# First attention of an eight-layer kernel: second half of the queries first, chunks projected and handed on inside the loop

## The chip, the core and the metric

The kernel runs on one core of a Trainium2 chip. The metric is the device time of one execution in microseconds; the median of three runs is given. Engines: TensorE (PE; its weight loads are PEld), VectorE (DVE), ScalarE (ACT), GpSimd (POOL) and SyncE (SP), which issues the DMAs.

## The reference, cut to what matters

Eight layers follow each other on x (2 batches of 1024 tokens, 128 features), each with a layer norm ahead of it and added back: four attentions and four feed-forward layers. The change lies in the first attention and in its hand-over to the first feed-forward layer.

```python
B, S, D = hidden_states.shape            # 2, 1024, 128
H, hd = (NUM_HEADS, HEAD_DIM)            # 16, 8
qkv = hidden_states @ w_attn + b_attn
scores = einsum('bhqd,bhkd->bhqk', q, k) * hd ** -0.5
# delta = key - query: -log(delta + 1) where delta > 0, 0 where 0, -inf where delta < 0
scores = scores + _power_law_mask(S)
attn = softmax(scores, axis=-1)
out = einsum('bhqk,bhkd->bhqd', attn, v) @ w_proj + b_proj
```

A query thus sees itself and the keys behind it. The second half of the queries (512 to 1023) sees only keys of the second half; the first half sees both. The next layer is a gated feed-forward: `silu(x @ wg.T) * (x @ wu.T) @ wd.T` with 384 hidden features.

## The kernel before

**Chunks and norm.** x lies in 4 chunks of 512 tokens (NC = 4, QC = 2 per batch). A `Norm` stands ahead of each layer: VectorE makes statistics (line 94, 98) and xn (line 106), GpSimd the root (lines 117, 119) and adds the output bias to x (line 136), TensorE turns xn (line 152), ScalarE copies it to xnT (line 165) and, for the feed-forward layer, rounds a high part (168), of which GpSimd makes the low part (125). `Part.ready` says after which addition the next norm may start; TensorE waits for all four chunks before it turns the first.

**Projection and stacks.** For each chunk TensorE projects q and k (line 449) and v (453). Q and k are split into three bf16 parts: high on ScalarE (575), rest on VectorE (638), mid on ScalarE (580), low on VectorE (653). SP stores them to DRAM (line 380, seven DMAs a chunk) and loads them back stacked, 48 rows a head (line 405, four DMAs a unit). One tile `parts` holds the parts of two chunks, so ScalarE waits for the stores of batch 0 before chunk 2. The order on SP's queue is: stores of chunks 0 and 1, stacks of units 0 to 2, stores of chunks 2 and 3, then the rows of maxima (line 394) and further stacks.

**Units.** A unit is 4 heads of one batch; there are 8 (UNITS). For each, the maximum over the keys of every query is found first: TensorE makes scores by query in 24 pieces (diagonal: lines 475, 481; behind: 487), VectorE reduces each (671). 8 of the pieces belong to the second half of the queries. VectorE then joins and splits the negated maxima into three bf16 parts (682 to 690), TensorE turns them (495), ScalarE copies them (619), SP moves them as rows under the stacked queries (394). Then the scores by key (line 511; logarithm of the weight added by 518, 519, or a mask by 523), exp on ScalarE (606), the weight on GpSimd for part of them (420), the product with V (540), the numerators copied (614), turned (549) and divided on VectorE (698, 701) into `o`, which is m.xn.

**The order of work** is one list, `schedule()`, that each engine follows for its own kinds. Its clock is the half: one pair of heads of one key block of one half of the queries. A unit has 12 groups (NG) and 24 halves (HALVES); the widths of its groups are 512 x5, 384, 256, 128 columns for the first half of the queries and then 512, 384, 256, 128 for the second. The product with V comes 7 halves after its scores. All 24 maxima of unit 0 stand ahead of the loop; those of unit u + 1 are spread over 24 halves that end 10 before unit u does (unit 1: 14 halves). Banks 4 to 6 of PSUM go round among scores by key, turned maxima and turned numerators.

**The end.** After the loop the four chunks are turned (560), copied (629), projected (565), added to x (712), and the norm of the next layer follows each. The next layer's gates are lines 765 and 766, their product on VectorE line 803; its weights are widened on ScalarE (752, 753) when the first attention has left it.

## Time and profile before

| what | us |
|---|---|
| median of 3 runs | 1101.84 |
| lowest, highest | 1100.96, 1110.02 |
| the profiled execution | 1110.22 |
| its span, first to last instruction | 1108.4 |
| mean granted clock of TensorE in it | 0.883 of full |

One execution was profiled. A row of the stage table gives the busy time of each engine in a stretch, with its instructions in brackets, and the granted clock (1.00 is 2.4 GHz, 0.50 is 1.2 GHz; between them the stretch had both). A row in order of time gives start and length in us; several instructions of one kind in a row are merged, with their count, and the bracket names the idle time ahead of them and what ended it.

### The profile page before, as it was taken

The numbers are of one execution on the slowest core, as the hardware profiler recorded it, in microseconds if no ns is written. First come the engines' busy times: TensorE is split into PE (matmuls) and PEld (weight loads), VectorE is DVE, ScalarE is ACT, GpSimd is POOL, SyncE is SP. The second block draws the span as 40 slices with busy tenths as digits, with TensorE's granted clock in tenths as the row PEclk, the third lists the DMA queues.
The fourth block names the chain that finished last, engine by engine and source line by source line (L and its number), as shares of the span: only waits on it lengthen the run. The fifth ranks groups of instructions, "written<-read, shape, count | busy, mean of one in ns | idle before, by whom it ended". The sixth has DMA issues, their size and how long they took to land. (4 is left out here: it accounts for less than half of the span.)

```text
span 1108.4 us, 17915 instructions
## 1 busy us (share of the span) xinstructions
PE 901.9 (81%) x6590; PEld 615.8 (56%) x6590; DVE 646.5 (58%) x1444; ACT 431.0 (39%) x1024; POOL 513.7 (46%) x462
## 2 busy tenths in 40 slices
PE   4559999999998877357899699995999996399993
PEld 2113334333333356255566588995896766289992
DVE  6756676767661065879687655778102666643334
ACT  2334665566555542113211285774344211032221
POOL 5435978887886832053222343655200001146661
PEclk9658999999997988758799698998899998599996
DMA  5700110111000000001000000211000000266775
GB/s 168 232 1 2 30 31 4 28 30 30 3 1 23 1 22 8 0 15 39 1 2 1 7 19 15 73 69 53 25 1 1 1 10 29 70 186 215 218 211 145
DMA packets 38747, 55.95 MB, mean 50 GB/s; under 512 B 6682, under 2 KB 26146, under 8 KB 38534
## 3 DMA queue, kind: packets, MB, share of 16 engines
q1 hardware_dynamic: 36166, 49.70, 14.8%
q0 software_dynamic: 2496, 5.12, 1.7%
q8 instruction: 54, 0.88, 0.3%
q14 instruction: 31, 0.25, 0.1%
HBM read 43.66 MB, written 10.94 MB: 49 GB/s over the span
## 5 line engine op out<-in xcount | busy, mean ns | idle before, releaser
L671 DVE TENSOR_REDUCE arena<-ps 128x2 f32<-128x1024 f32 (+2 forms) x192 | 177.4, 955 | 86.7 <-PE ps L487 55.4
L420 POOL TENSOR_TENSOR arena<-arena 128x1024 f32<-128x1024 f32 (+3 forms) x105 | 201.1, 1952 | 37.8 <-ACT arena L606 37.8
L606 ACT ACTIVATE arena<-ps 128x512 f32<-128x512 f32 (+3 forms) x320 | 138.7, 489 | 90.7 <-PE ps L519 56.1
L117 POOL TENSOR_SCALAR vareps<-meanvar 128x4 f32<-128x4 f32 x32 | 8.0, 250 | 213.7 <-DVE meanvar L98 213.7
L511 PE MATMUL ps<-arena 51*128 51x512 bf16 (+3 forms) x384 | 91.5, 348 | 18.0 <-ACT arena L606 7.1
L511 PEld LDWEIGHTS ps<-arena 51*128 51x128 bf16 x384 | 26.6, 94 | 107.1 <-ACT arena L606 61.4
L2084 PE MATMUL ps<-arena 128*128 128x128 f32 x624 | 78.2, 280 | 0.0
L152 PE MATMUL ps<-ident,xn 128*128 128x128 f32 x128 | 26.6, 358 | 59.2 <-DVE x L930 19.9
L2084 PEld LDWEIGHTS ps<-arena 128*128 128x128 f32 x624 | 74.8, 196 | 0.0
L420 POOL TENSOR_TENSOR xnT<-xnT,arena 128x1024 f32<-128x1024 f32 (+1 forms) x28 | 52.6, 1899 | 42.2 <-ACT xnT L606 42.2
L487 PE MATMUL ps<-arena 48*128 48x512 bf16 (+3 forms) x320 | 56.1, 347 | 17.5 <-DVE arena L671 14.8
L540 PE MATMUL ps<-arena 128*9 128x512 f32 (+3 forms) x640 | 69.0, 508 | 0.0
L1410 PEld LDWEIGHTS ps<-arena 128*128 128x128 f32 x512 | 63.8, 196 | 2.9
L1410 PE MATMUL ps<-arena 128*128 128x128 f32 x512 | 63.7, 279 | 0.0
L165 ACT ACTIVATE xnT<-ps 128x512 f32<-128x512 f32 x32 | 18.8, 595 | 110.6 <-PE ps L152 103.6
L2250 DVE TENSOR_TENSOR arena<-ps,arena 128x512 f32<-128x512 f32 x39 | 27.0, 692 | 58.2 <-PE ps L2084 57.3
L2044 POOL DMA_INDIRECT expert_rows<-arena x39 | 38.6, 989 | 40.9 <-ACT arena L2132 40.3
L2031 POOL DMA_INDIRECT arena<-token_rows,arena x39 | 38.0, 975 | 37.2 <-DVEq L2232 24.7
L152 PEld LDWEIGHTS ps<-ident,xn 128*128 128x128 f32 x128 | 20.2, 188 | 62.8 <-issue 43.4
L2118 ACT ACTIVATE arena<-ps 128x512 f32<-128x512 f32 x39 | 23.3, 597 | 71.0 <-PE ps L2084 70.9
L1461 ACT ACTIVATE arena<-arena 128x128 f32<-128x128 f32 x128 | 37.9, 297 | 31.2 <-DVE arena L1579 31.2
L1275 DVE TENSOR_TENSOR arena<-ps,arena 128x512 f32<-128x512 f32 x64 | 39.6, 681 | 17.3 <-PE ps L1157 17.3
(343 smaller groups left out, 2043.2 us busy)
## 6 DMA issues: line engine op xcount, KB each, us to landing
arena<-in_L_ffn_w SPq DMA_DIRECT2D x39, 512.0 KB, 3.7
arena<-scratch SPq DMA_DIRECT2D x32, 192.0 KB, 4.0
arena<-in_L_ffn_w SPq DMA_DIRECT2D x16, 256.0 KB, 3.3
scratch<-arena SPq DMA_DIRECT2D x12, 256.0 KB, 4.0
arena<-expert_rows SPq DMA_DIRECT2D x8, 256.0 KB, 5.0
scratch<-arena SPq DMA_DIRECT2D x4, 384.0 KB, 5.3
scratch<-arena SPq DMA_DIRECT2D x12, 128.0 KB, 4.1
x<-in_x SPq DMA_DIRECT2D x4, 256.0 KB, 3.8
```

The lines of the kernel that those rows point to most:

```text
L152: last = nc.tensor.transpose(m.ps[:, self.banks[n % len(self.banks)], j * P:(j + 1) * P], m.xn[:, n * TPC + j, :], m.ident[:, :])
L420: nc.gpsimd.tensor_tensor(e, e, weight[:, at:at + k].unsqueeze(1).broadcast_to([P, 2, k]), ALU.mult).then_inc(weighed, 1)
L487: mm = nc.tensor.matmul(m.ps[:, bank + e, 0:wd], qs[rows, u % BUFS, pair, at * P:(at + 1) * P], ks[rows, u % BUFS, pair, j:j + wd], start= ...
L511: mm = nc.tensor.matmul(m.ps[:, bank, 0:wd], ks[rows, u % BUFS, p, kt * P:(kt + 1) * P], qs[rows, u % BUFS, p, CH * qc:CH * qc + wd], star ...
L540: mm = nc.tensor.matmul(m.ps[PAD * h:PAD * h + HD + 1, 7, 0:wd], vones[:, b * TB + kt, u % G * GH + h, :], probs(u * NG + n)[:, h, 0:wd], ...
L606: nc.scalar.activation(probs(g)[:, 2 * p + e, 0:wd], m.ps[:, BANK[h, e], 0:wd], ACT.Exp, scale=SCALE).then_inc(exps, 1)
L671: nc.vector.tensor_reduce(out, scores, AX.X, ALU.max, negate=True).then_inc(max_set, 1)
L1275: nc.vector.tensor_tensor(at[:, t % 2, g, :].rearrange("p (j q) -> p j q", q=P), m.ps[:, g, :].rearrange("p (j q) -> p j q", q=P), causal[ ...
L1410: mm = nc.tensor.matmul(m.ps[:, 4 + n % 2, j * P:(j + 1) * P], hT[:, n % 2, f, j * P:(j + 1) * P], w2c[:, e % 2, f, :], start=False, stop= ...
L2031: nc.gpsimd.indirect_dma_start(xg[:, s % RING, :], None, m.token_rows, bass.IndirectOffsetOnAxis(ap=token_i[:, s:s + 1], axis=0),).then_in ...
L2044: nc.gpsimd.indirect_dma_start(m.expert_rows, bass.IndirectOffsetOnAxis(ap=target_i[:, s:s + 1], axis=0), y[:, s % RING, :], None,).then_i ...
L2084: mm = nc.tensor.matmul(m.ps[:, 2 * (s % 2) + half, f * P:(f + 1) * P], w_up[:, s % WBUFS, at + f * P:at + (f + 1) * P], xgT[:, s % 2, :], ...
```

## The change

- **Order of the queries.** Units 0 to 3 (batch 0) take the second half of the queries first, units 4 to 7 the first half. The pieces are listed with the second half first.
- **Maxima in halves.** For units 0 and 1 the maxima are split, turned, copied and moved in two turns (TURNS): first blocks 4 to 7, then 0 to 3. Only 8 pieces of unit 0 stand ahead of the loop. Its other 16 are due in halves 0 to 5, with the split at 6, the turning at 7 and the copy at 8. Unit 1: 2 pieces at 6, 4 at 7, 2 at 8 and 9, 16 in 10 to 21. Unit 2: all 24 in halves 22 to 37 (before 14 to 37). Later units as before.
- **Chunks inside the loop.** Four new kinds of work: turn_o, take_o, project, add. They use the rotating banks 4 to 6. Chunks 0 and 1 come after unit 3 (chunk 1 twelve halves later), chunk 2 after the first half of the queries of unit 7, chunk 3 at the end. With each addition VectorE does the statistics of that chunk and the normalisation of the chunk before it; GpSimd does the root 10 halves after the last product, or behind its last weighing.
- **Hand-over.** The next layer's chunk 0 is turned right behind the last product with V, and copied and split on ScalarE behind the last numerators. `wait_xnT` of that layer no longer waits for all chunks. The roots of its norm are taken as they come, at most one chunk ahead of the low part; that of chunk 3 falls between the low parts of chunks 1 and 2. The next layer's norm uses banks 3, 7, 6, 7.
- **Start.** The identity and three small loads (w, bqk, bv) are issued behind the first chunk of x, with semaphores of their own; TensorE waits for these and not for all seven loads. The first norm normalises each chunk behind the statistics of the next. The parts of batch 1 have a place of their own, in ring slots 2 and 3, so ScalarE doesn't wait for the stores of batch 0; it waits for the stores of batch 1 at group 3 instead.
- **SP's queue.** Stores of chunks 0 and 1, first three stores of chunk 2, stack of unit 0, the other stores, rows of unit 0, stacks of units 1 and 2, then rows and stacks as before.
- **Smaller.** `masked` lies in ring slot 0 and is made ahead of the logarithm, the scaling by 1 / SCALE goes from GpSimd to ScalarE, oT has a tile of its own.

```diff
     def vector(self, dve):
         while self.counted_stats < NC:
             self.statistics(dve, self.counted_stats)
+            if self.k == 0 and self.counted_stats >= 2:
+                self.normalise(dve, self.counted_xn)
...
         for c in range(NC):
-            ts = slice(c * TPC, (c + 1) * TPC)
-            pool.wait_ge(m.ln_var, 2 * self.value(c))
-            nc.gpsimd.tensor_scalar(m.vareps[:, ts], m.meanvar[:, ts, 1], LN_EPS, None, ALU.add).then_inc(m.ln_rstd, 1)
-            pool.wait_ge(m.ln_rstd, 2 * self.value(c) - 1)
-            nc.gpsimd.tensor_tensor(m.rstd[:, ts], m.vareps[:, ts], m.power[:, ts], ALU.pow).then_inc(m.ln_rstd, 1)
-        for c in range(NC):
+            while self.counted_roots < (min(c + 2, NC) if self.before.ahead else NC):
+                self.root(pool, self.counted_roots)
...
-        if self.turned == 0:
-            pe.wait_ge(*self.before.ready[NC - 1])
-            if self.k == 0:
-                pe.wait_ge(m.set_up, 2)
-                pe.wait_ge(m.consts_in, 16 * (2 + len(BIASES)))
+        if self.turned == 0 and not self.before.ahead:
+            pe.wait_ge(*self.before.ready[0 if self.k == 0 else NC - 1])
+        self.turn(pe, min(c + 2, NC))
...
+    ORDER = [tuple(range(QC)) if u >= (B - 1) * G else tuple(reversed(range(QC))) for u in range(UNITS)]
+    TURNS = [turn for u in range(UNITS) for turn in ([(u, TB - TPC, TB, 0, LATER), (u, 0, TB - TPC, LATER, NP)] if u < 2 else [(u, 0, TB, 0, NP)])]
...
-    def window(u):
-        return (0, HALVES - 10) if u == 1 else ((u - 1) * HALVES - 10, (u - 1) * HALVES + HALVES - 10)
+    def windows():
+        yield 0, LATER, NP, 0, 6
+        yield 1, 0, 2, 6, 7
+        yield 1, 2, 6, 7, 8
+        yield 1, 6, LATER, 8, 10
+        yield 1, LATER, NP, 10, HALVES - 2
+        yield 2, 0, NP, HALVES - 2, 2 * HALVES - 10
+        for u in range(3, UNITS):
+            yield u, 0, NP, (u - 1) * HALVES - 10, u * HALVES - 10
+
+    SPLIT_AT = [None, 6, 10, HALVES - 2] + [u * HALVES - 10 for u in range(2, UNITS)]
...
+    LATE = {c: 12 * (c == 1) for c in range(NC)}
+    ROOT_AT = {c: 2 * (u * NG + LAST[u][r]) + 2 * LAG + 10 + LATE[c] for c, (u, r) in FINISHED.items()}
...
-        yield from (("max", 0, n) for n in range(NP))
+        yield from (("max", 0, n) for n in range(LATER))
         yield from ((what, 0, 0) for what in ("split", "turn_max", "take_max"))
...
+                            for what, late in (("turn_o", 5), ("take_o", 6), ("project", 7)):
+                                due.setdefault(at + 2 * LAG + late + LATE[c], []).append((what, u, c))
+                            due.setdefault(at + 2 * LAG + 8 + LATE[c], []).insert(0, ("add", u, c))
...
+        for c in range(QC):
             for j in range(2):
+                store(c, j)
+        store(QC, 0)
+        stack(sp, 0)
+        store(QC, 1)
+        for c in range(QC + 1, NC):
+            for j in range(2):
+                store(c, j)
         maxima(sp, 0)
+        for u in range(1, BUFS):
+            stack(sp, u)
...
+    def maxima(sp, s):
+        u, lo, hi, _, _ = TURNS[s]
+        sp.wait_ge(mrows_set, s + 1)
+        if s and TURNS[s - 1][0] == u:
+
+            sp.wait_ge(s_mm, 2 * u * HALVES + 1)
...
+        def turn_outputs(u, c):
+            pe.wait_ge(o_set, u * QC + FINISHED[c][1] + 1)
+            bank = free_bank(("turn_o", u, c))
+            for j in range(TPC):
+                mm = nc.tensor.transpose(m.ps[:, bank, j * P:(j + 1) * P], o[:, c * TPC + j, :], m.ident[:, :])
+            mm.then_inc(o_turned, 1)
...
+            if what == "times_v" and (u, n) == (UNITS - 1, NG - 1):
+                turn_next(pe, 1)
...
+            if g == 3 and p == 0:
+                act.wait_ge(parts_out[B - 1], OUT)
...
+            if what == "take_num" and (u, n) == (UNITS - 1, QC - 1):
+                copy_next(act, 1)
...
+        def add(u, c):
+            dve.wait_ge(y_mm, c + 1)
+            dve.wait_ge(m.biased, norm.biased_value(c))
+            xs = m.x[:, c * TPC:(c + 1) * TPC, :]
+            nc.vector.tensor_tensor(xs, m.ps[:, BANK["project", u, c], :].rearrange("p (j d) -> p j d", d=D), xs, ALU.add).then_inc(x_done, 1)
+            after(dve, c)
```

## Rows read from the trace of the kernel before

**Rows 1.** the page: each engine's busy us (share of span) xinstructions

```profile
PE 901.9 (81%) x6590; PEld 615.8 (56%) x6590; DVE 646.5 (58%) x1444; ACT 431.0 (39%) x1024; POOL 513.7 (46%) x462
```

**Rows 2.** stages: stretch, length, PE PEld DVE ACT POOL busy, clock, DMA share, GB/s

```profile
39.60:63.00 23.40, 12.30 (x70) 3.23 (x68) 21.51 (x26) 1.98 (x3) 11.12 (x4) 0.59 0.50 160
63.00:70.70 7.70, 1.02 (x8) 0.74 (x8) 1.29 (x6) 2.30 (x2) 0.00 (x0) 0.50 0.01 3
70.70:92.00 21.30, 17.52 (x82) 5.42 (x84) 13.20 (x14) 9.61 (x18) 16.25 (x7) 0.59 0.00 1
92.00:105.00 13.00, 11.60 (x104) 4.73 (x100) 10.29 (x16) 5.42 (x15) 4.94 (x4) 1.00 0.00 1
143.90:182.50 38.60, 35.99 (x292) 14.26 (x290) 27.21 (x35) 22.37 (x52) 31.77 (x16) 1.00 0.09 22
386.70:403.40 16.70, 8.78 (x65) 7.61 (x61) 12.39 (x52) 6.99 (x12) 6.47 (x10) 0.86 0.10 26
```

**Rows 3.** order of time, the start; columns: start, length, engine, line, operation

```profile
13.23 1.97 PE L152 MATMUL ps<-ident,xn 128*128 128x128 f32 x8 [13.23 <-DMA arena<-in_L_attn_before]
...
15.03 2.65 PE L449 MATMUL ps<-xnT,arena 128*128 128x512 f32 x4
...
19.82 8.84 SPq L380 DMA_DIRECT2D scratch<-arena  x14
...
31.01 0.60 ACT L165 ACTIVATE xnT<-ps 128x512 f32<-128x512 f32 x1 [6.91 <-DMA scratch<-arena]
...
38.60 0.59 PE L475 MATMUL ps<-arena 128*128 128x512 bf16 x2 [1.08 <-DVE arena L650]
```

**Rows 4.** order of time, last maxima of unit 0 to first scores by key

```profile
54.83 1.04 PE L475 MATMUL ps<-arena 128*128 128x512 bf16 x2 [0.90 <-DVE arena L671]
...
62.94 0.39 DVE L682 TENSOR_TENSOR arena<-arena 128x28 f32<-128x28 f32 x2
...
66.61 43.70 SPq L394 DMA_DIRECT2D arena<-arena  x8
...
70.72 0.61 PE L511 MATMUL ps<-arena 51*128 51x512 bf16 x2 [5.18 <-DMA arena<-arena]
```

**Rows 5.** order of time of ScalarE, line 619 of unit 2 and unit 6

```profile
143.88 1.01 ACT L619 ACTIVATE arena<-ps 12x1024 bf16<-12x1024 bf16 x1 [1.90 <-PE ps L495]
...
296.43 1.01 ACT L619 ACTIVATE arena<-ps 12x1024 bf16<-12x1024 bf16 x1 [1.89 <-PE ps L495]
```

**Rows 6.** TensorE's busy time in four units by lines 487, 475, 481

```profile
143.90:296.40 152.50, 26.93 (x160) 1.00 0.09 22
...
143.90:296.40 152.50, 9.64 (x32) 1.00 0.09 22
...
143.90:296.40 152.50, 6.35 (x128) 1.00 0.09 22
```

**Rows 7.** order of time, last product with V to the next layer

```profile
384.39 2.34 PE L540 MATMUL ps<-arena 128*9 128x512 f32 x32
...
387.94 1.93 PE L560 MATMUL ps<-ident,xn 128*128 128x128 f32 x16
...
388.44 0.29 DVE L701 TENSOR_TENSOR xn<-ps,arena 128x128 f32<-128x128 f32 x1
...
389.71 1.06 PE L565 MATMUL ps<-arena 128*128 128x128 f32 x8
...
400.96 1.04 POOL L119 TENSOR_TENSOR rstd<-vareps,power 128x4 f32<-128x4 f32 x1
...
406.93 0.63 PE L765 MATMUL ps<-rounded 128*128 128x512 f32 x1
```

**Rows 8.** order of time of line 106 without and with GpSimd beside it

```profile
400.48 1.08 DVE L106 TENSOR_SCALAR xn<-x,meanvar,rstd 128x128 f32<-128x128 f32 x4
...
401.97 2.50 POOL L125 TENSOR_TENSOR rounded<-xnT,rounded 128x512 fp32r<-128x512 f32 x2
...
402.04 3.03 DVE L106 TENSOR_SCALAR xn<-x,meanvar,rstd 128x128 f32<-128x128 f32 x4 [0.47 <-POOL rstd L119]
```

More of the change, by code:

```diff
@@ L154, in wait_xnT, with copy @@
             self.turned += 1
-        pe.wait_ge(m.ln_xnT, self.value(c))
-        if self.split:
-            pe.wait_ge(m.x_low_set, self.split_value(c))
     def copy_xnT(self, act, c):
         nc, m = self.nc, self.m
-        while self.copied < min(c + 1, NC):
+        self.copy(act, min(c + 1, NC))
+    def copy(self, act, n_copied):
+        nc, m = self.nc, self.m
+        while self.copied < n_copied:
             n = self.copied
@@ L312, in schedule @@
                     due.setdefault(at, []).append(("exp", u, (n, p)))
+        for s in range(1, len(TURNS)):
+            for what, late in (("split", 0), ("turn_max", 1)):
+                due.setdefault(SPLIT_AT[s] + late, []).append((what, TURNS[s][0], s))
         for at, pieces in PIECES_AT.items():
@@ L384, in sync, with store @@
-        maxima(sp, 0)
-        for u in range(1, UNITS):
-            maxima(sp, u)
-            if u + 2 < UNITS:
-                stack(sp, u + 2)
-    def maxima(sp, u):
-        sp.wait_ge(mrows_set, u + 1)
+        def store(c, j):
+            sp.wait_ge(low_set, 2 * c + j + 1)
+            for part, slot, step, n in RUNS[j]:
+                dst = scratch[j, slot:slot + step * (n - 1) + 1:step, :, c * CH:(c + 1) * CH].rearrange("s f t -> f s t")
+                src = parts_of[c // QC][:, part, j, c % 2 * CH:(c % 2 + 1) * CH].unsqueeze(1).broadcast_to([P, n, CH])
+                sp.dma_start(dst, src).then_inc(parts_out[c // QC], 16)
@@ new lines, in sync, with first_loads @@
+        for c in range(QC):
+            for j in range(2):
+                store(c, j)
[5 more added lines that the diff above has]
+                store(c, j)
+        maxima(sp, 0)
+        for u in range(1, BUFS):
+            stack(sp, u)
+        for s in range(1, len(TURNS)):
+            maxima(sp, s)
+            if s >= 3 and s < UNITS:
+                stack(sp, s)
+    def first_loads(sp):
+        sp.dma_start(w[:, :, :], A["L0_attn_w"]).then_inc(first_in, 16)
+        sp.dma_start(bqk[:, :], A["L0_attn_bqk"]).then_inc(first_in, 16)
+        sp.dma_start(bv[:, :], A["L0_attn_bv"].broadcast_to([P, D])).then_inc(first_in, 16)
@@ L692, in divide, with split_maxima @@
-        def divide(u, qc):
-            k = u * QC + qc
+        def split_maxima(u, s):
+            _, lo, hi, _, last = TURNS[s]
+            dve.wait_ge(max_set, NP * u + last)
+            mine = negmax[:, u % 2, 0, :, lo:hi]
+            part = lambda p: nparts[:, u % 2, lo:hi, :].rearrange("q i (h p) -> q h i p", p=3)[:, :, :, p]
+            left = nrest[:, :, lo:hi]
+            done = SPLIT[s]
+            if u >= 2:
+                dve.wait_ge(n_turned, TURNED[u - 2])
+            for n, first, end in JOINS[s]:
+                nearer = negmax[:, u % 2, 0, :, first:end]
+                nc.vector.tensor_tensor(nearer, nearer, negmax[:, u % 2, n, :, first:end], ALU.min).then_inc(nsplit, 1)
+                done += 1
+                dve.wait_ge(nsplit, done)
+            nc.vector.tensor_copy(part(0), mine).then_inc(nsplit, 1)
+            dve.wait_ge(nsplit, done + 1)
+            nc.vector.tensor_tensor(left, mine, part(0), ALU.subtract).then_inc(nsplit, 1)
+            dve.wait_ge(nsplit, done + 2)
+            nc.vector.tensor_copy(part(1), left).then_inc(nsplit, 1)
+            dve.wait_ge(nsplit, done + 3)
+            nc.vector.tensor_tensor(part(2), left, part(1), ALU.subtract).then_inc(nparts_set, 1)
@@ L2437, in after, with root, turn, copy @@
             return following[id(norm)].after if id(norm) in following else lambda dve, c: None
+        def root(norm):
+            return following[id(norm)].root if id(norm) in following else lambda pool, c: None
+        def turn(norm):
+            return following[id(norm)].turn if id(norm) in following else lambda pe, n: None
+        def copy(norm):
+            return following[id(norm)].copy if id(norm) in following else lambda act, n: None
         block = ctx.enter_context(nc.Block())
@@ L2483, in _ @@
                     part.before_norm["scalar"](act)
-                part.scalar(act)
+                if part.ahead:
+                    part.scalar(act, copy(norm))
+                else:
+                    part.scalar(act)
         @block.gpsimd
@@ L2493, in _ @@
                 norm.gpsimd(pool, m.bias_of.get(part.bias))
-                if part.gpsimd:
+                if part.ahead:
+                    part.gpsimd(pool, root(norm))
+                elif part.gpsimd:
                     part.gpsimd(pool)
```

311 lines of the change are left out of this document (157 added, 154 removed).

## The prediction, made before the change was run

> **What bounds the kernel now.** I read the page first, then the stage table, then the order of time. On the page TensorE is busy 81% of the span and no other engine over 58% [rows 1], but an average over eight layers says little about one. The stage table gives the first attention, 0 to 387 us, piece by piece [rows 2]. The reader should see three kinds of stretch. First a start in which TensorE mostly waits: from 39.6 to 63.0 it is busy 12.3 of 23.4 us at a granted clock of 0.59 while VectorE is busy 21.5, and from 63.0 to 70.7 it does 1.0 us of work. Then a steady part: 143.9 to 182.5 is one unit of the loop, TensorE busy 36.0 of 38.6 us at clock 1.00, VectorE 27.2, GpSimd 31.8. There TensorE's order of work sets the pace, so whatever is added to TensorE costs its own length. Last a tail from 386.7 to 403.4, where TensorE is busy 8.8 of 16.7 us, until the next layer's first gate. The change aims at the start and at the tail, and pays in the steady part.
>
> The order of time shows what the start waits for. TensorE transposes nothing before 13.23 us, when the last of the weight loads has landed; the first projection is at 15.03. The 14 stores of batch 0 are issued from 19.82 on; ScalarE then stands 6.91 us until they have landed at 31.01, because the parts of batch 1 go to the same tile; the stacks wait for the same, and the first scores by query run at about 38.6 [rows 3]. Then come all 24 maxima of unit 0. The last eight (second half of the queries) begin on TensorE at 54.83 and the splitting begins at 62.94; from there to the first scores by key at 70.72 it is 7.8 us, 4.1 of them from the issue of the rows to their landing [rows 4].
>
> **The start, step by step.** The first projection now needs chunk 0 and 1 of x, the identity and three small loads. Chunk 1 of x is issued four DMAs later; VectorE then does statistics 0 and 1 and the first two normalisations, which puts the projection at about 12 to 13, 2.5 us before 15.03 (an estimate; 0 to 3.5). The stores of batch 0 shift with it and land at 28.5. The stack of unit 0 is now 4 DMAs and not 12, but 3 stores of chunk 2 stand ahead of it on SP's queue (0.63 us each to issue: 8.84 for 14 [rows 3]). Batch 1's projection, no longer stopped, ends near 30. First scores by query: 34.0 (33 to 36), against 38.6. Eight maxima: 62.94 - 54.83 = 8.1, split at 42.1. Split to first scores by key: 7.8, less 1.2 because four blocks are turned and copied in place of eight, 6.6. First scores by key: 48.7, which is 22.0 us earlier. The logarithm table, now with two GpSimd passes ahead of the Ln, is finished near 41 and hidden.
>
> This gain is mostly work put off, not removed. The other 16 maxima of unit 0 now stand inside the first six halves. The nearest rows: the first 16 alone took 54.83 - 38.6 = 16.2 us, and the stretch 70.7 to 92.0, with 14 maxima and some eight full halves, took 21.3. I take 18.5. Then split, turning, copying and landing, twice on the path now, 6.8. Half 8 (first half of the queries) starts at 48.7 + 18.5 + 6.8 = 74.0. Six maxima of unit 1 lie in that wait.
>
> **From half 8 to the last product with V.** Before, 70.7 to 386.7 is 316.0 us. What stands ahead at 74.0 is less by the scores by key of halves 0 to 7. A unit takes (296.43 - 143.88) / 4 = 38.1 us [rows 5], of which maxima are (26.9 + 9.6 + 6.4) / 4 = 10.7 of TensorE [rows 6], so 27.4 are left for 9216 columns; halves 0 to 7 have 2560, hence 7.6. Their last three products with V are still to come, +1.9 (four of such mixed widths took 2.34 [rows 7]). Six maxima of unit 1 are done, -3.2 (two diagonals and four narrow pieces of the 24 that make 10.7). The slow clock: 21.3 us at 0.59 lose 8.7 [rows 2]. TensorE waits before half 8 as it did before half 0, so it begins slow again, but with 18 maxima in the next 14 halves and not 24 it is held up less by VectorE; I allow half of the loss, 4.4. So 316.0 - 7.6 + 1.9 - 3.2 - 8.7 + 4.4 = 302.8, end at 376.8, 9.9 us earlier than 386.7.
>
> Against that stands what is moved in. Turning a chunk is a quarter of 1.93 us of TensorE, projecting one 1.06 [rows 7], 1.6 together with gaps; for chunks 0 and 1 that is 3.3 in all, and for chunk 2, among the last four products with V, 2.0 with the wait for ScalarE's copy. TensorE also waits in order for the division and for a bank that the addition frees: 1.0 for both chunks (0 to 4). Unit 2's 24 maxima go into 16 halves in place of 24: VectorE needs some 24 us there and TensorE 27, so 1.0 (0 to 4). The normalisation of chunk 0 now falls among GpSimd's products. On VectorE four of these took 1.08 us with GpSimd idle and 3.03 beside two GpSimd instructions of 512 columns, 1.25 each [rows 8]; GpSimd's products here are up to 1024 columns wide, so 2.5 each. If each of the four waits for a whole one it is 10 us; VectorE has 11 us free per unit (27.2 of 38.6 busy) and TensorE is two maxima ahead, so I take 3.0 (0 to 8). Chunk 1 and 2 are normalised when VectorE has nothing else. Statistics, additions and roots are a few us in VectorE's and GpSimd's free time; without that cover they would cost 4 more. Sum 10.3. The last product with V ends at 376.8 + 10.3 = 387.1, practically where it was.
>
> The Trainium skill, "SBUF — State Buffer", section "Who interferes with whom", says that VectorE and GpSimd lock a shared port pair for a whole instruction and that tensor_scalar can take it. The row of 3.03 against 1.08 agrees. By that rule alone the term would be the full 10 and not 3, and the sum 7 worse.
>
> **The tail.** Call the last product's end E, 386.7 before. The division ends at E+2.0 [rows 7]; one chunk, not four, is turned (0.5), copied (0.6, as [rows 3]) and projected (1.06): E+4.6 with the gaps between engines. The next layer turns its chunk 1 by E+5.6, chunk 0 being turned and copied behind E already. Its first gates run at about E+5.5, where before they ran at 403.4, E+16.7 [rows 2]. But VectorE holds the gating back: it must first normalise chunk 3, whose root GpSimd computes only after splitting chunks 0 and 1, the second after copy and rounding at E+7.0: 1.25 [rows 8] to E+8.3, root 1.3 (two steps, the second 1.04 [rows 7]) to E+9.6, normalisation 1.1 [rows 8] to E+10.8, first gating 0.7. The third gate, which waits for it, starts at E+11.6. Before, it started at 406.93, E+20.2. Gain 8.6; the slow clock that held there before may or may not return, 0.4. Together -9.0. From there the next layer runs as before.
>
> **Sum.** +0.4 at E and -9.0 in the tail: -8.6 us. The profiled execution took 1110.22 (span 1108.4 and 1.8 around it), so it would become 1101.6. It is the slowest of the runs shown; taken off their median, 1101.84, the forecast is 1093.
>
> **The rivals.** Each time is the median plus its difference.
> (a) Early start kept: the clock is full right at half 8 (-4.4), and bank waits, port and squeeze cost nothing (-5.0): -18, so 1084. For it: GpSimd and VectorE have gaps in every unit. Against it: TensorE's 7.7 us at clock 0.50 before 70.7 is repeated before half 8.
> (b) The rows of the maxima come late: on SP's queue they stand behind 11 stores of batch 1; 14 such stores took from 19.82 to 31.01 [rows 3], so 11 take 8.8. If they still move when the rows are issued near 44, everything slides by up to 7: 1100. Against it: begun at 32, they should be out by 41.
> (c) Slower: TensorE stays at half clock after half 8, starved by VectorE. Up to half 22 there are 27 us of TensorE's work at full clock; at half clock they cost 27 more, not 4.4: +14, so 1116. It decides from 26 us of half clock on, where the gain of 8.6 is gone. For it: 39.6 to 92 ran at 0.50 to 0.59. Against it: from 92 on the clock was 1.00 with maxima still interleaved [rows 2].
> The Trainium skill, "TensorE: Matmul & The Clock Gate", section "What's actually happening", has half rate as the default that activity releases; the rows at 0.50 in TensorE's wait agree, and it speaks for (c) where the waits are.
>
> **How the numbers follow.** Forecast 0.42, by itself 1087 to 1099; (a) 0.27; (b) 0.19; (c) 0.12. About 1% is what a measurement tells from no change: faster is below 1090.8, slower above 1112.9. Faster: (a) and three tenths of the forecast, 0.40. Slower: most of (c), 0.10. Same: 0.50. The range runs from 4 below (a) to 8 above (b), 1080 to 1108; it leaves out (c) and the ends of (a).
>
> **What would show it.** First scores by key at 47 to 51 and not 70.7; half 8 at 72 to 77, with a slow clock ahead of it; the last product with V at 383 to 391; the next layer's first gate some 5 to 6 us behind it and the third at 11 to 12. Four normalising instructions of chunk 0 lasting well over 1.08 us in unit 5 would show the port. The forecast is wrong if half 8 comes after 80, if the last product moves by over 5 us either way, or if the gates do not follow within 8.

## The result, and the profile after

The changed kernel took 1151.0 us (median; 1147.5 to 1158.9) beside 1104.5 us for the kernel before (1101.0 to 1110.0): 1.040 of it, 95% interval 1.035 to 1.045. It is slower by 46 us, where a forecast of 1093 and a range up to 1108 had been given. The profiled execution took 1149.9 us, with a span of 1147.9. The experiments below were timed in four groups, in which the median of the kernel before was 1106.6 to 1114.5 us, so only the ratios are compared across them.

The page's engine row, to be held against [rows 1]:

```profile
PE 912.2 (79%) x6590; PEld 615.9 (54%) x6590; DVE 672.4 (59%) x1454; ACT 433.0 (38%) x1027; POOL 509.9 (44%) x461
```

TensorE's busy time has risen by 10 us with the same number of instructions, and GpSimd's has not risen. VectorE's busy time rose by 26 us, from 646.5 to 672.4, though all it got in addition is ten tiny instructions: some of its instructions have become longer. The stage table of the kernel after, for the first four stretches of [rows 2] and one in the middle of the loop:

```profile
39.60:63.00 23.40, 11.85 (x73) 4.43 (x74) 14.51 (x21) 5.24 (x9) 6.45 (x3) 0.65 0.42 112
63.00:70.70 7.70, 6.67 (x36) 3.06 (x32) 6.48 (x9) 2.37 (x7) 3.11 (x3) 0.50 0.00 0
70.70:92.00 21.30, 14.53 (x82) 3.80 (x81) 18.10 (x21) 6.33 (x14) 9.97 (x5) 0.58 0.01 1
92.00:105.00 13.00, 11.27 (x83) 4.24 (x86) 9.70 (x12) 6.91 (x14) 7.47 (x4) 0.87 0.01 3
...
195.00:205.00 10.00, 6.51 (x35) 2.72 (x36) 6.07 (x8) 1.01 (x1) 2.75 (x2) 0.52 0.01 2
```

The dead stretch at 63 to 70.7 is filled, as intended. What is new is a stretch such as 195 to 205, in the middle of what was the steady part at clock 1.00: granted clock 0.52 and TensorE busy 6.5 of 10 us. Where the time goes shows when one sets down the copy of the last numerators of each unit on ScalarE (line 614 before, the `take_num` entry) in order of time, in us; e1, e14 and e15 are experiments told below:

```
unit                       0      1      2      3      4      5      6      7
before                  127.4  165.2  203.9  241.5  279.6  319.3  361.3  386.8
after                   127.8  176.3  226.0  274.8  328.7  367.8  407.7  436.5
e1  (split guard)       122.2  164.4  201.9  240.2  292.1  330.0  366.6  395.6
e14 (both guards)       119.9  162.4  199.9  238.2  281.5  321.7  361.9  392.2
e15 (outputs behind)    122.6  164.7  202.2  240.6  278.2  316.1  356.1  386.1
```

Each row is one profiled execution. Two programs that are the same until long after unit 0 (the kernel after and e12 below) end unit 0 at 127.8 and 131.2, so differences under some 3 us in a single row say little. In the kernel after, unit 0 ends where it did; units 1, 2 and 3 then lose 11 us each, unit 4 loses 16, and after that the distance stays at 46 to 50. One of those units in order of time, by engine (start, length, engine, line, operation, with the idle time before it in brackets). First VectorE, which reduces two maxima (line 753) and then splits those of unit 3 (lines 767 to 776):

```profile
186.63 2.36 DVE L753 TENSOR_REDUCE arena<-ps 128x2 f32<-128x1024 f32 x2 [0.16 <-PE ps L560]
189.03 4.17 DVE L767 TENSOR_TENSOR arena<-arena 128x28 f32<-128x28 f32 x2
193.23 2.33 DVE L770 CAST arena<-arena 128x32 bf16<-128x32 f32 x1
195.59 2.24 DVE L772 TENSOR_TENSOR arena<-arena 128x32 f32<-128x32 f32 x1
197.87 0.24 DVE L774 CAST arena<-arena 128x32 bf16<-128x32 f32 x1
198.14 0.30 DVE L776 TENSOR_TENSOR arena<-arena 128x32 bf16<-128x32 f32 x1
```

then GpSimd, its products with the weights:

```profile
186.19 4.67 POOL L490 TENSOR_TENSOR arena<-arena 128x1024 f32<-128x1024 f32 x2
190.83 4.63 POOL L490 TENSOR_TENSOR xnT<-xnT,arena 128x1024 f32<-128x1024 f32 x2
195.43 2.33 POOL L490 TENSOR_TENSOR arena<-arena 128x1024 f32<-128x1024 f32 x1
```

and TensorE's turning of the maxima with ScalarE's copy of it:

```profile
198.49 1.02 PE L568 MATMUL ps<-arena 128*12 128x128 bf16 x8 [8.43 <-DVE arena L776]
...
199.55 1.01 ACT L700 ACTIVATE arena<-ps 12x1024 bf16<-12x1024 bf16 x1 [8.29 <-PE ps L568]
```

A cast of 128x32 takes 0.24 us once GpSimd is still, at 197.87, and 2.33 us at 193.23. Each of the four instructions before 197.8 ends when one of GpSimd's products ends: about 190.8, 193.2, 195.5 and 197.8. The split lasts 9.4 us; TensorE stands 8.4 us and then works at half clock. The same split in the kernel before, in order of time (its first joining of the maxima, and TensorE's turning):

```profile
177.54 3.09 DVE L682 TENSOR_TENSOR arena<-arena 128x28 f32<-128x28 f32 x2
...
181.83 0.61 PE L495 MATMUL ps<-arena 128*12 128x128 bf16 x8 [0.51 <-DVE arena L690]
```

There the whole split lasted 4.2 us, beside GpSimd products of 1.26 us (128x512), TensorE waited 0.51 us and ScalarE 2.59. The reduction of line 753, whose input is in `ps`, has its usual length beside GpSimd (1.18 us each), and GpSimd's products keep theirs: it is VectorE that waits.

Why it is so only now: the split of unit u+1's maxima is due at half 14 of unit u. In the old order of the queries that is the last group of the first half, 128 columns wide, behind two of 384 and 256. With the second half first, half 14 lies in the middle of the five groups of the first half that are 512 columns wide, and GpSimd's products there are all 128x1024. For the splits of units 2 and later the diff leaves that half as it was; it moves the wide groups under it.

### The profile page after: what moved, and what is told of

Same layout as the page of the kernel before. It is cut to its first block and busy times, and to the rows that moved or that the text cites. A ratio compares the mean times of both kernels' runs of the same rounds, so it can differ in the third digit from the quotient of the medians.

```text
span 1147.9 us, 17952 instructions
## 1 busy us (share of the span) xinstructions
PE 912.2 (79%) x6590; PEld 615.9 (54%) x6590; DVE 672.4 (59%) x1454; ACT 433.0 (38%) x1027; POOL 509.9 (44%) x461
## 5 line engine op out<-in xcount | busy, mean ns | idle before, releaser
L490 POOL TENSOR_TENSOR arena<-arena 128x1024 f32<-128x1024 f32 (+3 forms) x105 | 195.1, 1882 | 94.2 <-ACT arena L687 93.8
L687 ACT ACTIVATE arena<-ps 128x512 f32<-128x512 f32 (+3 forms) x320 | 135.4, 480 | 134.0 <-PE ps L593 64.5
L490 POOL TENSOR_TENSOR xnT<-xnT,arena 128x1024 f32<-128x1024 f32 (+1 forms) x28 | 59.2, 2130 | 40.2 <-ACT xnT L687 40.2
L615 PE MATMUL ps<-arena 128*9 128x512 f32 (+3 forms) x640 | 71.9, 524 | 0.0
L109 DVE TENSOR_SCALAR xn<-x,meanvar,rstd 128x128 f32<-128x128 f32 x128 | 50.6, 462 | 2.8 <-POOL rstd L136 2.8
```

What stands on the lines that cost most here:

```text
L109: last = nc.vector.tensor_scalar(m.xn[:, t, :], m.x[:, t, :], m.meanvar[:, t, 0:1], m.rstd[:, t:t + 1], ALU.subtract, ALU.mult)
L490: nc.gpsimd.tensor_tensor(e, e, weight[:, at:at + k].unsqueeze(1).broadcast_to([P, 2, k]), ALU.mult).then_inc(weighed, 1)
L615: mm = nc.tensor.matmul(m.ps[PAD * h:PAD * h + HD + 1, 7, 0:wd], vones[:, b * TB + kt, u % G * GH + h, :], probs(u * NG + n)[:, h, 0:wd], ...
L687: nc.scalar.activation(probs(g)[:, 2 * p + e, 0:wd], m.ps[:, BANK[h, e], 0:wd], ACT.Exp, scale=SCALE).then_inc(exps, 1)
```

## The experiments

Two theories stood at the outset. P (the port): the splits are long because each of their short instructions waits for a whole wide product of GpSimd. Its rivals: the loop has become longer by its own order (maxima of two units, banks, the outputs inside it), which would stay if the splits were short again. Later came O (the split's place inside its half of the schedule: ahead of the piece and the product with V that are due in the same half, or behind them) and the price of chunk 0's normalisation.

**e1: the splits with GpSimd held back.** The kernel after; GpSimd, three halves ahead of each split inside the loop, waits for it to be finished.

```
+        splits = {SPLIT_AT[s] - 3: s for s in range(1, len(TURNS))}
         for h in range(UNITS * HALVES):
+            if h in splits:
+                pool.wait_ge(nparts_set, splits[h] + 1)
```

> The changed kernel, but GpSimd waits, three halves before each split inside the loop is due, until VectorE has finished that split. Nothing else moves. Theory P (port): in units 1 to 3 of the changed kernel the six short instructions of a split last 7 to 9.6 us because each stands behind a product of GpSimd of up to 2.3 us; TensorE idles for the turned maxima and comes back at half clock. With GpSimd held, each split should last about 1.5 us, the idle before the turned maxima should fall from 5 to 8 us to under 3, and about 9 us should come back for each of the three units and some 5 for unit 0: 1115 to 1125 in place of 1151. Theory O (order): the loss comes from the order itself, narrow groups first or the bank rotation, and TensorE would stand elsewhere; the split gets short but the time stays within 10 us of 1151, or grows because GpSimd now idles.

Measured: 1.001 of before (0.997 to 1.004), so 43 us are gone, more than the 26 to 36 that were expected. The same split in order of time of VectorE, and of GpSimd's next product:

```profile
173.09 2.36 DVE L756 TENSOR_REDUCE arena<-ps 128x2 f32<-128x1024 f32 x2 [0.16 <-PE ps L563]
175.48 0.39 DVE L770 TENSOR_TENSOR arena<-arena 128x28 f32<-128x28 f32 x2
175.90 0.24 DVE L773 CAST arena<-arena 128x32 bf16<-128x32 f32 x1
176.18 0.21 DVE L775 TENSOR_TENSOR arena<-arena 128x32 f32<-128x32 f32 x1
176.43 0.24 DVE L777 CAST arena<-arena 128x32 bf16<-128x32 f32 x1
176.70 0.30 DVE L779 TENSOR_TENSOR arena<-arena 128x32 bf16<-128x32 f32 x1
...
177.08 2.35 POOL L490 TENSOR_TENSOR arena<-arena 128x1024 f32<-128x1024 f32 x1 [1.87 <-DVE arena L779]
```

1.5 us in place of 9.4, for 1.9 us in which GpSimd stands, which it can afford. Nothing of the order, the banks or the pieces was changed, so the rivals of P fall for all but a few us.

**e4: wide products under the splits of the kernel before.** The kernel before, with the window's end, and so the split, of units 2 to 7 moved from half 14 to half 8 of the unit before, which has 512 columns in the old order. The 24 maxima of unit 2 thereby lie in 18 halves in place of 24.

```
     def window(u):
-        return (0, HALVES - 10) if u == 1 else ((u - 1) * HALVES - 10, (u - 1) * HALVES + HALVES - 10)
+        end = lambda v: HALVES - 10 if v == 1 else (v - 1) * HALVES + 8
+        return (0 if u == 1 else end(u - 1), end(u))
```

> The kernel before with one thing moved: the maxima of units 2 to 7 end, and their split is due, at half 8 of the unit before, where the groups are 512 columns wide, and not at half 14. No other order, no chunks in the loop. Theory P: the splits last 6 to 10 us in place of 1.5 to 4, in six units, TensorE idles 4 to 8 us before each turning and each unit costs 6 to 10 us more: 1140 to 1165 against 1104. Theory O: the place of the split is of no matter, only unit 2's maxima are squeezed a little: 1102 to 1112.

Measured: 1.044 of before (1.036 to 1.053), as long as the changed kernel with none of the change in it. ScalarE's copy of the turned maxima, in order of time (units 3 and 4; six such waits of 4.7 to 6.4 us in all, 1.9 to 2.9 in the kernel before):

```profile
193.06 1.01 ACT L620 ACTIVATE arena<-ps 12x1024 bf16<-12x1024 bf16 x1 [6.35 <-PE ps L496]
...
247.37 1.01 ACT L620 ACTIVATE arena<-ps 12x1024 bf16<-12x1024 bf16 x1 [6.37 <-PE ps L496]
```

e1 takes the loss away and e4 makes such waits from nothing: P is shown from both sides. Its size is shown by e1 alone, for the loop of e4 ended 52 us later by another path. 9 us were lost by the end of unit 0, where no split had moved (3.5 of them ahead of the first scores by key), and unit 2 took 54.3 us in place of 38.6. After its wait of 4.68 us TensorE worked without a gap and the clock stayed low all the same:

```profile
200.00:220.00 20.00, 20.00 (x102) 6.93 (x102) 7.58 (x8) 7.24 (x19) 10.85 (x7) 0.50 0.00 1
```

The wait of 4.71 us one unit later was over with the clock back at 1.00 within 6 us, and that unit took 44.8. What set the two apart no run shows.

**e3: reversed order in units 0 and 1 alone.** One line; from unit 2 on the splits lie under narrow groups again.

```
-    ORDER = [tuple(range(QC)) if u >= (B - 1) * G else tuple(reversed(range(QC))) for u in range(UNITS)]
+    ORDER = [tuple(range(QC)) if u >= 2 else tuple(reversed(range(QC))) for u in range(UNITS)]
```

> The changed kernel with the second half of the queries first in units 0 and 1 only; units 2 and 3 take the first half first, as 4 to 7 do. Theory P: the split of unit u + 1 is due at half 14 of unit u; with the first half of the queries first the groups there are 256 and 128 columns wide, with the second half first 512. So the splits that lie in units 2 and 3 should fall from 9.6 us to 2 to 4, the one in unit 1 stays long, and units 2 and 3 each give back about 10 us: 1128 to 1134. Theory O with maxima squeezed into unit 2 as the cause: units 2 and 3 have the same number of maxima per half in either order, so nothing or little comes back, 1145 to 1151.

Measured: 1.024 (1.017 to 1.032). The waits for unit 3's and 4's maxima shrank from 8.3 and 8.5 us to 2.4 and 3.1, and units 2 and 3 took 41.3 and 41.5 us in place of 49.6 and 48.9. So 1.5% came back, but 2.4% was left and had to come from the units before and from elsewhere.

**e7a: old order everywhere, new start and new end.** The kernel after with the old order, old pieces, old windows and one split per unit; the earlier loads and projection, the outputs inside the loop and the hand-over stay.

```
-    ORDER = [tuple(range(QC)) if u >= (B - 1) * G else tuple(reversed(range(QC))) for u in range(UNITS)]
+    ORDER = [tuple(range(QC)) for u in range(UNITS)]
...
-    SPLIT_AT = [None, 6, 10, HALVES - 2] + [u * HALVES - 10 for u in range(2, UNITS)]
+    SPLIT_AT = [None] + [u * HALVES - 10 for u in range(1, UNITS)]
```

> The changed kernel with the order of queries, of the pieces and of the splits of the kernel before: all 24 maxima of unit 0 ahead of the loop, one split a unit. The new start (loads, projection, own place for batch 1's parts), the chunks inside the loop and the hand-over stay. Both theories agree on the loop without the reversal: what is left are the start (first scores by query 1 us earlier), the tail (10 us less from the last product with V to the end of the next layer) and what the chunks and the normalisation of chunk 0 cost inside the loop, which was some 12 us in the changed kernel. If that cost is the port alone, as P has it, the sum is near zero: 1098 to 1110. If chunks inside the loop cost more than they save, 1112 or more.

Measured: 1.017 (1.011 to 1.024), where about 1.00 was expected. Each of its units 1 to 3 took 41 us, against 38 before, with narrow products and no output yet. TensorE at one of its splits:

```profile
188.12 0.28 PE L588 MATMUL ps<-rounded 128*128 128x128 f32 x1
190.23 0.61 PE L563 MATMUL ps<-arena 128*12 128x128 bf16 x8 [1.83 <-DVE arena L771]
190.77 0.60 PE L543 MATMUL ps<-arena 128*128 128x512 bf16 x2
```

and the stage just after it:

```profile
190.00:195.00 5.00, 4.77 (x32) 1.33 (x32) 1.40 (x2) 1.70 (x3) 0.00 (x0) 0.68 0.01 4
```

Before, the piece and the product with V stood ahead of the turning and covered the split. In the kernel after, `schedule()` enters the split and the turn first in their halves, so TensorE meets the turn with nothing left to do: an edit in the diff that I had not seen as one. That gave theory O.

**The place in the half.** Four kernels bear on O; the edit in all of them moves these lines from ahead of the pieces to behind them.

```
         for s in range(1, len(TURNS)):
+            for what, late in (("split", 0), ("turn_max", 1)):
+                due.setdefault(SPLIT_AT[s] + late, []).append((what, TURNS[s][0], s))
             due.setdefault(SPLIT_AT[s] + 2, []).insert(0, ("take_max", TURNS[s][0], s))
```

On e7a (the text below says "e4 here" and means e7a):

> e4 here is the earlier kernel with the old order of the queries, the new start and the new hand-over (1.0173 of before), in which every split was followed by 2.3 us of waiting and some 5 us at a clock of 0.66. Its one edit more: the split and the turn of the maxima stand at the end of their half, behind the piece and the product with V, as in the kernel before. Theory O (the place in the half costs 2 to 3 us for each of seven units): 0.998 to 1.003. If the place costs nothing and something else in the loop is slower: 1.017 still.

Measured: 1.0125 (1.0075 to 1.0174). Its units 1 to 3 took 37.8, 38.6 and 37.7 us, those of the kernel before to 0.1 us, so O holds for the units: 3 us each. TensorE waits 0.51 us and not 1.83 at the same split:

```profile
189.46 1.04 PE L609 MATMUL ps<-arena 128*9 128x512 f32 x8
191.01 0.61 PE L562 MATMUL ps<-arena 128*12 128x128 bf16 x8 [0.51 <-DVE arena L770]
```

But of the 19 us that e7a lost only 5 come back, which the two intervals don't tell from none: unit 0 ended 3.7 us later than in e7a and unit 4, with the outputs, took 51.2 us in place of 44.8. On the kernel after itself:

> The kernel after with this one edit: the split and the turn of the maxima stand at the end of their half. The splits stay under the wide products and last 7 to 9.6 us. Theory O: TensorE has one piece and one product with V (about 2 us) to do before it waits, so 2 to 3 us less for each of six splits: 1.023 to 1.030 of before. Theory P alone (only the port): TensorE's wait ends with the split whatever lies before it, 1.04 still.

Measured: 1.039 (1.034 to 1.044), nothing gained in the whole, but by two effects that cancel. From the end of unit 0 to the last numerators it is 298.1 us, 10.6 less than in the kernel after, 1 to 3 of them in each of units 1 to 6. And unit 0 ends 12.7 us later, at 140.5. Some 6 us of that lie at unit 0's own second turn: its split now stands behind two pieces and its turning behind four more and a product with V, so the rows are issued 30.0 us behind the first scores by key and not 23.6, and half 8, the first to need them, begins 33.9 us behind them and not 27.5:

```profile
88.02 0.61 PE L584 MATMUL ps<-arena 51*128 51x512 bf16 x2 [4.53 <-DMA arena<-arena]
```

With both guards:

> The kernel after with three edits: GpSimd waits for each split three halves ahead of it (as in e1), GpSimd waits at half 120 until chunk 0 is normalised, and the split and the turn of the maxima stand at the end of their half in the schedule, behind the piece and the product with V, as in the kernel before. If all three stalls are what the kernel after lost: the first guard has given 43 us, the one for chunk 0 gives 8 to 10 (its four operations took 7.23 us instead of about 2, and TensorE stood 5 us and then ran at 1.2 GHz until about 330 us), the place in the half at most 1 us per unit on top of the first guard: 0.985 to 0.993 of the kernel before on the same chip. If the guard for chunk 0 only moves the wait to GpSimd and the place does nothing: 1.00, as e1.

Measured: 1.006 (1.003 to 1.009), worse than with the guards alone (e6, below). Half 8 again begins 33.4 us behind the first scores by key, in e6 26.5, and unit 0 ends 7.6 us later, half of the 15.4 by which the loop does. In the later units ScalarE waits 1.1 to 2.2 us for the turns instead of at most 1.6. So O holds, 2 to 3 us a unit, where the split is not guarded, and moving the place has a price of 6 to 7 us in unit 0 wherever the maxima come in two turns. And with reversed order in two units only:

> Reversed order in units 0 and 1 alone, so that the splits from unit 3 on lie under narrow products; the splits and turns at the end of their half, as before; both guards of e6. The kernel with the reversed order in two units alone was 1.0243 of before. Taking away its waits for the turned maxima (2.4 to 4.7 us in five units) and the 8 us at chunk 0's normalisation gives 15 to 20 us: 1.005 to 1.010. If the end of the loop is worth its 10 us in full it comes out at 0.995 to 1.000.

Measured: 1.000 (0.997 to 1.004), between its two expectations, though half 8 comes 33.5 us behind the first scores by key here too: e3's 2.4% is the splits, chunk 0's normalisation and the waits at the place in the half, net of that, in shares that this run doesn't part.

**Chunk 0's normalisation.** In the kernel after, VectorE and GpSimd in order of time in unit 4 (line 109 normalises):

```profile
311.62 7.23 DVE L109 TENSOR_SCALAR xn<-x,meanvar,rstd 128x128 f32<-128x128 f32 x4
...
311.72 4.75 POOL L490 TENSOR_TENSOR xnT<-xnT,arena 128x1024 f32<-128x1024 f32 x2 [4.50 <-ACT xnT L687]
316.42 2.34 POOL L490 TENSOR_TENSOR arena<-arena 128x1024 f32<-128x1024 f32 x1
...
320.04 0.50 PE L560 MATMUL ps<-arena 48*128 48x384 bf16 x2 [6.82 <-DVE arena L753]
```

Four instructions last through three products, and TensorE stands 6.8 us, since the maxima queue behind them on VectorE. A guard, one wait, holds GpSimd back at half 120 until they are done:

```
+            if h == 120:
+                pool.wait_ge(m.ln_xn, NC + 1)
```

On top of e1:

> e1 and the guard for chunk 0's normalisation, the place in the half as in the kernel after. Against e1 (1.0007 of before) this prices chunk 0's normalisation alone. If it costs what the trace of the kernel after shows (TensorE idle 5 us and slow for 10 more): 0.991 to 0.993. If the wait only moves: 1.00.

Measured: 0.997 (0.994 to 1.001), between its two expectations. The same kernel again, timed side by side with the two kernels at the end of this section:

> The kernel of e6 again, beside the other two rungs on one chip, since e6 and e11 were timed in different calls and their profiles stand the other way round (e6 reaches the second normalisation behind the attention 3 us earlier than e11). If handing over inside the loop gains what its trace shows: 3 us less than the top rung. If it costs, as the medians said: 5 to 8 us more.

Measured: 0.995 (0.993 to 0.997). The four instructions take 1.08 us again (e14, order of time of VectorE):

```profile
273.02 1.08 DVE L109 TENSOR_SCALAR xn<-x,meanvar,rstd 128x128 f32<-128x128 f32 x4
```

Two stage rows of 24 us, in each of which the normalisation begins 7 to 8 us in, show what the stall does to TensorE's busy time and clock; first e14, then e1:

```profile
265.00:289.00 24.00, 21.17 (x172) 8.91 (x172) 17.69 (x34) 13.97 (x31) 19.75 (x12) 1.00 0.14 34
```

e1:

```profile
268.00:292.00 24.00, 16.70 (x120) 6.37 (x120) 17.71 (x24) 9.67 (x22) 18.66 (x12) 0.72 0.16 34
```

Unit 4 took 51.9 us in e1 and 43.3 in e14 and e6: the stall cost 8.6 us there. Of the whole time 4 to 7 us came back (1.001 against 0.997 and 0.995). The guard alone, on the kernel after:

> The kernel after with the guard for chunk 0's normalisation alone (GpSimd waits at half 120); the splits stay unguarded. With e1 and e6 it fills the square. If the two stalls add up: the kernel after less 8 to 9 us, 1.031 to 1.033 of before. If it does nothing by itself: 1.039.

Measured: 1.036 (1.029 to 1.043). Unit 4 took 46.8 us in place of 53.9, but the loop ended only 1.9 us earlier, since this execution was already 3.4 us behind at the end of unit 0, where the two programs are the same. The interval covers both the 8 to 9 us that were expected and next to nothing.

**Is the guard worth something by itself?** The kernel before with the split guard and nothing else:

> The kernel before with the guard alone: GpSimd waits for each split three halves ahead of it. It separates a repair from a gain that any order of the queries would have. In the kernel before a split lies under products of 0.7 and 1.3 us, takes 3 to 4 us, and ScalarE waits 1.7 to 2.6 us for the turned maxima. If only the wide products made the splits dear: 0.997 to 1.003. If the guard gains whatever the width: seven times 1 to 2 us, 0.987 to 0.993.

Measured: 0.995 (0.990 to 0.999), between its two expectations. So the guard gains about 6 us (1 to 11) in the old order too, under narrow products. The change with its stalls guarded (e6, e14) must be compared with this kernel, and then is worth nothing that was measured.

**What the outputs inside the loop earn.** Three steps between "all inside" (e14) and "all behind" (e15), all with the guard for the splits; e14 has the guard for chunk 0 besides, which the others don't need. All four chunks projected, normalised and handed over behind the loop, timed first without the other two:

```
-    LATE = {c: 12 * (c == 1) for c in range(NC)}
+    LATE = {0: 89, 1: 91, 2: 5, 3: 0}
...
-                turn_next(pe, 1)
...
-                copy_next(act, 1)
```

> e1 (guard for the splits, 1.0007 of before) with all four chunks projected, normalised and handed over behind the loop, as in the kernel before. It prices what is done inside the loop. Unit 4 of e1 took 51.9 us against 38.1 before: 8 us of it the normalisation of chunk 0, 5 us the outputs of chunks 0 and 1. If that is their whole price the loop ends 13 us earlier, and the end gives back its 10 us: 0.997 of before (0.994 to 1.000). If handing over inside the loop hides nothing that matters at the end: 0.989.

Measured: 0.991 (0.987 to 0.994). The same kernel again, side by side with e14 and e13:

> The kernel of e11 again, beside the other two: 0.988 to 0.994 of before if e11 stands; 0.995 to 0.999 if the two calls differed by their chip's state and not by the kernels.

Measured: 0.993 (0.990 to 0.996), beside 0.995 (0.993 to 0.997) for e14, which does all inside and comes out between its two expectations. The step between, outputs inside and normalisation behind (all roots behind the loop, no early turn, and VectorE normalises chunks 0 and 1 after chunk 2 is added):

> e1 (guard for the splits) with chunks 0 and 1 turned, projected and added inside the loop as in the kernel after, but all square roots, normalisation and the hand-over behind the loop. Middle rung between e11 (nothing inside the loop, 0.991 of before) and e6 (everything inside, both guards, 0.997 of before). If the normalisation and its guard inside the loop are what costs: 0.989 to 0.991, unit 4 longer than in e11 by the outputs' 3 to 5 us and the end shorter. If the outputs inside the loop are what costs: 0.995 to 0.998, unit 4 as in e6 (43 us), and nothing gained behind the loop.

Measured: 0.9995 (0.997 to 1.002), worse than the worse of its expectations (0.995 to 0.998). The three stand in the order of their traces. The outputs lengthen unit 4 from 37.6 us (e15) to 42.5 (e13), 5 us. From the last numerators' copy to the last chunk turned for the second normalisation behind this one, on TensorE, is 126.3 us in e15 (386.13 to 512.46), 128.4 in e13 (388.43 to 516.82) and 122.3 in e14 (392.23 to 514.50): the hand-over inside the loop gives back 4 to 6 us. One execution of each fixes this loosely: the kernel of e15, profiled as e11, took 130.6, and that of e14, as e6, 123.3. The difference of 0.2% between e14 and e15 can't be told from nothing, and that between e6 and e11 (0.997 and 0.991) leans the same way; the outputs inside the loop earn no more than they cost.

## Why the prediction was wrong, step by step

**What bounds the kernel** was read rightly: TensorE's order sets the pace, and whoever makes it wait sets the end. The sentence "VectorE has 11 us free per unit" was true and did not help: the loss comes from what TensorE waits for in order, and VectorE's mean busy time doesn't show that.

**The start** was put 3 to 5 us too early. First projection 12.5 (said 12 to 13). The stores were issued at 20.3 and not 2.5 us ahead of 19.82, as the sum had it, since four normalising instructions of VectorE ahead of them, at 14.21, took 4.00 us beside three additions of the bias by GpSimd (3.72 us); first scores by query 37.4 (said 34.0), split 45.5 (42.1), first scores by key 51.9 (48.7, before 70.7), half 8 at 79.4 (74.0). In order of time of TensorE:

```profile
37.39 1.01 PE L548 MATMUL ps<-arena 128*128 128x512 bf16 x2 [5.40 <-DMA arena<-scratch]
...
51.92 0.61 PE L585 MATMUL ps<-arena 51*128 51x512 bf16 x2 [4.66 <-DMA arena<-arena]
...
90.79 0.59 PE L568 MATMUL ps<-arena 128*12 128x128 bf16 x4 [5.59 <-DVE arena L776]
```

The last of these rows is unit 1's first split, which began at 81.86 and took 9 us under four products back to back; it ate what the start had left, and unit 0 ended at 127.8 against 127.4. With the guard (e1, e14, e15) unit 0 ended 5 to 7.5 us early, and then unit 1 took 42 us and not 38: where the squeeze of maxima stands, put at 1.0, 4 to 5 are lost (no run parts them further). What is left of the start's gain after unit 1 is 0.5 to 3 us in these three, and nothing in e6.

**The loop** is the step that failed. "From half 8 to the last product with V" took the unit of the kernel before, 38.1 us [rows 5], and subtracted and added work; the splits inside those 38.1 us were carried over at their old length. Reversing the order put products of 2.3 us under them in place of 0.7 to 1.3, so the row could not be carried over. The term for longer splits was zero and measured 43 us (e1 against the kernel after), of the 58 between the forecast of 1093 and the 1151 measured. The prediction's own sign of being wrong, a last product moved by over 5 us, came with 50. No rival held it either: the slow clock of (c) was 0.58 in 70.7 to 92, hardly other than 0.59 before, and what it cost later followed the splits and not the maxima that (c) spoke of.

The Trainium skill, "SBUF — State Buffer", section "Who interferes with whom", says that VectorE instructions with two SBUF inputs, and casts and tensor_scalar in some forms, contend with GpSimd, that tensor_reduce never does, and that the blocked side waits for the whole instruction. The rows at 186 to 198 us agree for the cast, the operations with two inputs and the reduction, and the four tensor_scalar of chunk 0 (7.23 us against 1.08) for the rest. The prediction cited this section for four instructions of chunk 0 and did not ask which other VectorE instructions of the loop it holds for, though the six of the split stand in the diff.

**Chunk 0's normalisation** was put at 3.0 (0 to 8), by VectorE's free time, against 10 if each of the four waited for a whole product. It measured 8.6 (e1 to e14 in unit 4): the four took 7.23 us, through three products, and TensorE's lead was used up 1.6 us after the first of them began. The 10 were the better guide; the free time didn't help, since the maxima queue behind the four.

**The other terms inside the loop.** Outputs of chunks 0 and 1 with bank waits: 4.3 said, 5 measured (e13 against e15). The place of the splits in their halves was not seen: 3 us per unit with the old order (e7a and its variant), 2 to 3 in units 2 and 3 of the kernel after (e8).

**The tail** was right in its steps and nearly in size. E is 436.5 in the kernel after; TensorE's gates behind it, in order of time, to be held against [rows 7]:

```profile
435.61 0.84 PE L615 MATMUL ps<-arena 128*9 128x256 f32 x16
...
443.27 0.78 PE L854 MATMUL ps<-rounded 128*128 128x512 f32 x1
...
449.39 0.50 PE L854 MATMUL ps<-rounded 128*128 128x512 f32 x1 [2.38 <-DVE arena L892]
```

First gate at E+6.8 (said 5.5, before 16.7), third at E+12.9 (said 11.6, before 20.2): 7.3 gained where 8.6 was said. The clock was 0.74 in the 13 us behind E; in e6, where it was 0.99, the gates came at E+5.7 and E+11.7, as forecast. From E to the end of the span it is 711.4 us against 721.6, 10.2 shorter, and -9.0 was the term; but that agreement proves little, for in e9, whose program behind E is that of the kernel before, it is 713.5.

With both guards in place the sum stands nearly as written: the last numerators are copied at 387.0 in e6 (392.2 in e14) against E at 387.1, and 0.995 to 0.997 of before against 0.992. Part of this is luck: the guard for the splits brings about 6 us that the sum doesn't hold (e9), while the start and the squeeze cost 6 to 9 more than it said (an estimate, from the rows and unit times above). The forecast was wrong mainly by one omitted term of 43 us.

## What to carry to other kernels

When an edit reorders work on one engine, go through every short instruction of the engine that was seen to wait for it (here VectorE for GpSimd) and look up what will now run beside it; a stage's time per unit can't be carried over if the partner's instructions grow. A chain of n tiny VectorE instructions beside back-to-back GpSimd instructions cost up to one of the latter for each (here four of six waited), and where TensorE waited for the chain, its clock fell too; letting GpSimd wait cost it 1.9 us in the chain shown, 4.3 in one of e14, and saved 43 us here. Work moved from behind a loop into it is paid at the pace of the loop's bound engine: here 5 us of outputs bought 4 to 6 us at the end, and the whole was no faster. Before a change of place inside the order is called worthless, its gain and its price are looked for unit by unit: in e8 they cancelled.

## What the runs showed of the chip that was not expected

How exactly the waiting is in whole instructions: casts and two-input operations of 0.21 to 0.24 us took 2.24 to 2.33 us, one GpSimd product of 2.33 us for each, one behind the other, while GpSimd lost nothing. And how much a wait of TensorE costs beyond its length: the unit of the kernel after that contains the 8.4 us wait shown above took 49.6 us against 38.6, 11.0 us more, with a granted clock of 0.52 in the 10 us that hold its end. A wait of 1.8 us in e7a was followed by 0.68 over 5 us; the wait of 0.51 us in its variant left the clock at 1.00. No fixed factor comes of this: in e4 a wait of 4.68 us was followed by over 30 us at 0.50 with TensorE busy throughout, one of 4.71 us by a return to 1.00 within 6 us.
